# The landmark stage's first normalisations, turns and image 0's projections, moved into the last pair of the Fourier stage

## The chip, the cores and the metric

One Trainium2 chip, one core of it. The metric is the device time of one execution of the kernel in microseconds (us), as the median of several runs. The profile comes from one execution; its times count from the start of its span.

## The reference

```python
# x: (8, 16, 16, 192); a hybrid of four layers. Around the change:
x = x + _L1_conv_ref(_gn(x), ...)         # Fourier mixing of a group-normalised image
t = _to_tokens(x)                         # 8 images of 256 tokens, 192 channels
t = t + _L2_attn_ref(_ln_t(t), ...)       # landmark attention, per image

def _L1_conv_ref(x, w1, w2, b1, b2):
    xf = jnp.fft.rfft2(x, axes=(1, 2), norm='ortho')      # in 8 blocks of 24 channels
    o1 = softshrink(xf @ w1 + b1)                         # complex, block-wise
    o2 = softshrink(o1 @ w2 + b2)
    return irfft2(o2, s=(H, W), norm='ortho') + x

def _L2_attn_ref(x, Wqkv, bqkv, Wo, bo, Wconv):
    q, k, v = jnp.split(x @ Wqkv + bqkv, 3, axis=-1)      # 12 heads of 16
    q_l, k_l = pool(q), pool(k)                           # 16 landmarks: means over segments
    kernel_1 = softmax(q @ k_l.T * scale)
    kernel_2 = softmax(q_l @ k_l.T * scale)
    kernel_3 = softmax(q_l @ k.T * scale) @ v
    x_out = kernel_1 @ _iterative_pinv(kernel_2) @ kernel_3
    x_out = x_out + v_conv                                # depthwise, 33 taps along the tokens
    return x_out @ Wo + bo
```

`_ln_t` is a layer norm over the 192 channels without weights. Behind the landmark attention come a layer of routed experts, a full attention and another layer of experts.

## The kernel before

The kernel is a row of stages, each a block of instruction lists for the five engines: TensorE (PE), VectorE (DVE), ScalarE (ACT), GpSimd (POOL) and SyncE (SP, which issues most of the DMAs). At the end of a block all engines meet at a barrier, and nothing of the next block starts before it. Within a block each engine works through its list in order and waits on semaphores. The residual stream X, 8 images of 2 tiles of 128 tokens, stays in SBUF for the whole run.

**The Fourier stage**, `l1_afno`, takes the images in four pairs. In each, TensorE does `forward` (the transform), `first` and `second` (the two block-wise layers), `second_rest`, and `backward` (the inverse transform) of both images. ScalarE copies the spectrum (`spectrum`) and does the two halves of the first soft-shrink (`shrunk`). VectorE joins them (`hidden`), does the second soft-shrink (`result`, `result_rest`) and adds the residual (`residual`). Between these, the first three pairs carry the group-norm statistics of the pair to come: `gn.mean` and `gn.variance` on TensorE into the banks psM and psV, `gn.square` and `gn.root` on ScalarE, `gn.total` to `gn.norm` on VectorE. The last pair has none of this, and psM and psV lie unused in it. Behind each residual add stand the layer-norm statistics that the landmark attention needs, `stats.vector` (mean and variance, VectorE) and `stats.gpsimd` (the reciprocal root, GpSimd). GpSimd also makes the residual sum XS (L1689). SP loads the weights of the landmark stage (`early`) during this stage.

**The feature stage**, `l2_features`, runs over the images one by one as a software pipeline, c = -2 to 8 on TensorE and ScalarE. For each image: normalisation (`norm`, DVE L2098), turn (transposes, PE L1942) with a copy out (`turned_in`, ACT L2067), projections to queries, keys and values (PE L1953, L1960) with bias copies (`projected`, ACT L2046; `values`, DVE L2107), landmark means (`means`, DVE L2116 to L2121), logits (`logits`, PE L1970 and L1975), the convolution with rows of a Toeplitz matrix (`convolve`, PE L1990), softmaxes, and products. At c = -2 only image 0 is turned. At c = -1 image 0 is projected and image 1 is turned. At c = 0 image 1 is projected, and then come the logits of image 0. The order on TensorE is:

```python
for c in range(-2, B + 1):
    if has(c + 1): project(c + 1, queries)
    if has(c):     logits(c); convolve(c); turn_keys(c)
    if has(c + 2): turn(c + 2)
    if has(c):     landmarks(c)
```

The stage begins with SP's load of the Toeplitz rows `toep` (L1917), GpSimd's fills of the two value tiles VZ (L1924), and VectorE's `norm(0)`, `norm(1)` and the scaled head mask `hms` (L2153). Behind it come `l2_inverse` (the iterated inverse) and the route stage with the experts' weights. Each stage's semaphores are cleared by GpSimd at its end.

Of the kernel before, what the change touches and what calls it, by code (L numbers as in the profile page):

```python
# [17 lines left out]
T = HH * WW  # L18
P = 128
# [1622 lines left out]
def l1_afno(nc, G, w, consts, transfers, gn):  # L1642
# [5 lines left out]
    with Stage(nc, "l1") as st:  # L1648
# [8 lines left out]
        stats = LnStats(st, G, 1e-5)  # L1657
# [11 lines left out]
        def _(sp):  # L1669
# [8 lines left out]
            early.start(sp)  # L1678
            early.finish(sp)

        @block.gpsimd
        def _(pool):
            stats.init(pool)

# [13 lines left out]
            for u in range(2):  # L1698
                stats.gpsimd(nc, pool, B - 2 + u, u)

        @block.tensor
        def _(pe):
# [55 lines left out]
            for p in range(NP):  # L1758
                forward(2 * p)
                forward(2 * p + 1)  # L1760
                if p + 1 < NP:
                    gn.mean(pe, psM, p + 1)
                first(2 * p)
                first(2 * p + 1)
                if p + 1 < NP:
                    gn.variance(pe, psV, p + 1)
                second(2 * p)
                second(2 * p + 1)
                second_rest(p)
                backward(2 * p)  # L1770
                backward(2 * p + 1)

        @block.scalar
        def _(act):
# [18 lines left out]
            for p in range(NP):  # L1793
                spectrum(2 * p)
                spectrum(2 * p + 1)
                if p + 1 < NP:
                    gn.square(act, 2 * p + 2)
                    gn.square(act, 2 * p + 3)
                shrunk(2 * p, 0)
# [3 lines left out]
                if p + 1 < NP:  # L1803
                    gn.root(act, p + 1)

        @block.vector
        def _(dve):
# [31 lines left out]
            def residual(i):  # L1839
# [42 lines left out]
def l2_features(nc, G, w, consts, transfers):  # L1882
# [6 lines left out]
    with Stage(nc, "l2p") as st:  # L1889
        W, qkb, vb, hm = (G["marks"][n] for n in ("W", "qkb", "vb", "hm"))  # L1890
        hms = st.sb("hms", [CH, HB])
        toep = st.sb("toep", [P, NH, TW])
        two = lambda name, shape: [st.sb(f"{name}{u}", shape) for u in range(2)]
        xn, xT = two("xn", [P, TI, C]), two("xT", [CH, 2, T])
        QT, KT, VZ = two("QT", [CH, 2, T]), two("KT", [CH, 2, T]), two("VZ", [P, TI, NH, 2 * HD])
# [6 lines left out]
        normed, turned, xT_done, cleared, tp_in = st.sems("normed turned xT_done cleared tp_in")  # L1902
        q_mm, q_done, k_mm, k_done, v_mm, v_done, sum_done, lm_done = st.sems("q_mm q_done k_mm k_done v_mm v_done sum_done lm_done")
# [12 lines left out]
        def _(sp):  # L1916
            sp.dma_start(toep[:, :, :], rows(G["band"], 0, [TW, P], [P * TW, NH], [1, TW])).then_inc(tp_in, 16)  # L1917
# [13 lines left out]
        def _(pe):  # L1931
            reach = ((0, 0, P + KS // 2), (1, P - KS // 2, T))

            def turn(i):
                u = i % 2
                pe.wait_ge(normed, TI * (i + 1))
                if i >= 2:
                    pe.wait_ge(xT_done, i - 1)
                ps = both(psT[u][0:CH, :])
                for t in range(TI):  # L1940
                    for k in range(2):
                        mm = nc.tensor.transpose(ps[:, k, t * P:(t + 1) * P], xn[u][:, t, k * CH:(k + 1) * CH], ident[:, :])  # L1942
                mm.then_inc(turned, 1)

            def project(i, between):
                u = i % 2
                pe.wait_ge(xT_done, i + 1)
                for ps, m0, done, mm_done in ((psQ, 0, q_done, q_mm), (psK, 2, k_done, k_mm)):
                    if i:
                        pe.wait_ge(done, i)  # L1950
                    for a in range(2):
                        for k in range(2):
                            mm = nc.tensor.matmul(ps[0:CH, a * T:(a + 1) * T], W[:, k, (m0 + a) * CH:(m0 + a + 1) * CH], xT[u][:, k, :], start=(k == 0), stop=(k == 1))  # L1953
                    mm.then_inc(mm_done, 1)
                between()
                if i:
                    pe.wait_ge(v_done, i)
                for t in range(TI):
                    for k in range(2):
                        mm = nc.tensor.matmul(psV[:, t * C:(t + 1) * C], xT[u][:, k, t * P:(t + 1) * P], W[:, k, 2 * C:], start=(k == 0), stop=(k == 1))  # L1960
                mm.then_inc(v_mm, 1)
# [16 lines left out]
            def convolve(i):  # L1978
                u = i % 2
                if i == 0:  # L1980
                    pe.wait_ge(tp_in, 16)
# [40 lines left out]
            for c in range(-2, B + 1):  # L2022
# [9 lines left out]
                if has(c + 2):  # L2032
                    turn(c + 2)
# [4 lines left out]
        def _(act):  # L2038
            def projected(i):
                u = i % 2  # L2040
                if i >= 2:
                    act.wait_ge(l3_mm, i - 1)
                for ps, dst, b0, mm_done, done in ((psQ, QT, 0, q_mm, q_done), (psK, KT, 2, k_mm, k_done)):
                    act.wait_ge(mm_done, i + 1)
                    for a in range(2):
                        ev = nc.scalar.activation(dst[u][:, a, :], ps[0:CH, a * T:(a + 1) * T], ACT.Identity, bias=qkb[:, b0 + a:b0 + a + 1])  # L2046
                    ev.then_inc(done, 1)
# [14 lines left out]
            def turned_in(i):  # L2062
                u = i % 2
                act.wait_ge(turned, i + 1)
# [1305 lines left out]
```

## Time and profile before

| | us |
|---|---|
| median of 3 runs | 1144.66 |
| lowest and highest | 1143.66, 1145.24 |
| profiled execution | 1144.88 |
| its span | 1142.5 |
| TensorE busy | 1001.3 |
| VectorE busy | 579.1 |
| ScalarE busy | 420.7 |
| GpSimd busy | 286.9 |

The span reaches from the first to the last instruction of the profile; what lies around it is 2.4 us. A busy time is a sum over the engine's instructions. In rows of the profile, PEld is TensorE's load of weights, which overlaps its matmuls; PEclk is the clock granted to TensorE, 1.00 for 2.4 GHz and 0.50 for 1.2 GHz; an idle time in brackets names what ended it.

### The profile page before, as it was taken

How to read it: one execution, taken by the hardware profiler on the slowest of the kernel's cores; microseconds unless marked ns; L12 is line 12 of the kernel's file. 1: busy time of each engine (PE TensorE's matmuls, PEld its weight loads, DVE VectorE, ACT ScalarE, POOL GpSimd, SP SyncE). 2: the span in 40 equal slices, each digit the busy share in tenths (PEclk: the TensorE clock that was granted, in tenths of full speed). 3: DMA queues.
4: the chain of work that ended last, by engine and by line, in shares of the span. 5: the costliest groups of instructions: out<-in, count | busy, mean ns of one | idle time of the engine just before them, and what ended most of it. 6: DMA issues, size and time to landing. Idle time of an engine off the chain costs nothing. (4 is left out here: it accounts for less than half of the span.)

```text
span 1142.5 us, 20449 instructions
## 1 busy us (share of the span) xinstructions
PE 1001.3 (88%) x7506; PEld 760.0 (67%) x7507; DVE 579.1 (51%) x1394; ACT 420.7 (37%) x853; POOL 286.9 (25%) x399
## 2 busy tenths in 40 slices
PE   6796899999699999799799839999949799993996
PEld 5686687887457678688599715666637445573775
DVE  3754455554312375556475654444459487744221
ACT  3665055455332323344352101111107366641332
POOL 4464230111210021100000262555432311103242
PEclk9885899999799999899898859999979899995999
DMA  8543763330001220200003710111134443414670
GB/s 92 120 111 117 169 168 84 82 82 3 3 23 62 65 55 1 56 1 2 1 1 81 233 32 28 50 49 49 42 112 105 118 120 99 147 43 171 206 206 15
DMA packets 103318, 91.58 MB, mean 80 GB/s; under 512 B 25905, under 2 KB 95095, under 8 KB 102590
## 3 DMA queue, kind: packets, MB, share of 16 engines
q1 hardware_dynamic: 93161, 77.15, 25.2%
q0 software_dynamic: 5632, 11.07, 3.6%
q10 hardware_dynamic: 4437, 2.17, 0.7%
q8 instruction: 57, 0.93, 0.4%
q14 instruction: 31, 0.25, 0.1%
HBM read 64.44 MB, written 29.70 MB: 82 GB/s over the span
## 5 line engine op out<-in xcount | busy, mean ns | idle before, releaser
L1305 DVE TENSOR_REDUCE l0a_nmax<-l0a_psS 98x2 f32<-98x392 f32 x96 | 54.3, 567 | 54.9 <-PE l0a_psS L1120 50.8
L2778 ACT ACTIVATE l2e_H<-l2e_psH 128x512 f32<-128x512 f32 x40 | 21.7, 595 | 130.2 <-PE l2e_psH L2740 130.2
L895 ACT ACTIVATE l3a_PT<-l3a_psST 128x512 f32<-128x512 f32 x96 | 54.6, 595 | 31.5 <-PE l3a_psST L806 30.8
L1255 ACT ACTIVATE l0a_PT<-l0a_psST 98x392 f32<-98x392 f32 x96 | 47.2, 497 | 42.2 <-PE l0a_psST L1162 41.8
L2758 PEld LDWEIGHTS l2e_psY<-W2T,l2e_HT 128*128 128x128 f32 x320 | 51.5, 190 | 15.9 <-issue 15.8
L2701 POOL DMA_INDIRECT ys<-l2e_Y,result_of x40 | 42.0, 1050 | 72.3 <-DVE l2e_Y L2805 66.2
L2758 PE MATMUL l2e_psY<-W2T,l2e_HT 128*128 x320 | 57.3, 332 | 1.3 <-DVE l2e_Y L2805 0.8
L941 DVE TENSOR_REDUCE l3a_nmax<-l3a_psS 128x2 f32<-128x512 f32 x48 | 33.0, 687 | 24.6 <-PE l3a_psS L776 24.5
L2805 DVE COPY l2e_Y<-l2e_psY 128x384 f32<-128x384 f32 x20 | 11.2, 558 | 65.1 <-PE l2e_psY L2758 65.1
L2737 PE MATMUL l2e_psH<-W1T,l2e_XT 128*128 x80 | 41.3, 640 | 2.8 <-issue 2.0
L2696 POOL DMA_INDIRECT l2e_X<-xn,token_at x40 | 39.2, 980 | 17.1 <-issue 17.1
L806 PE MATMUL l3a_psST<-l3a_QS,l3a_KS 99*128 99x256 bf16 x192 | 36.4, 273 | 0.4 <-ACT l3a_PT L895 0.3
L941 DVE TENSOR_REDUCE l3a_nmax<-l3f_psL 128x2 f32<-128x512 f32 x48 | 32.8, 684 | 5.2 <-PE l3f_psL L776 5.2
L1257 ACT ACTIVATE l0a_PT<-l0a_psST 120x360 f32<-120x360 f32 x48 | 22.1, 470 | 31.8 <-PE l0a_psST L1170 29.3
L1554 PE MATMUL l0m_psY<-early,l0m_hT 128*128 128x192 f32 x192 | 32.2, 328 | 1.7 <-ACT l0m_hT L1584 1.7
L1308 DVE TENSOR_REDUCE l0a_nmax<-l0a_psS 120x1 f32<-120x312 f32 x48 | 22.9, 480 | 20.6 <-PE l0a_psS L1129 19.0
L1554 PEld LDWEIGHTS l0m_psY<-early,l0m_hT 128*128 128x128 f32 x192 | 31.1, 190 | 2.3 <-ACT l0m_hT L1584 2.3
L1087 POOL CAST l0a_mp<-l0a_nmax 128x20 bf16<-128x20 f32 x12 | 2.4, 199 | 120.0 <-DVE l0a_nmax L1308 120.0
L2974 PE MATMUL l3e_psY<-l3w_B,l3e_HT 128*128 128x192 f32 x192 | 32.5, 327 | 0.0
L1584 ACT ACTIVATE l0m_hT<-l0m_psH,early 128x512 f32<-128x512 f32 x24 | 15.2, 683 | 45.6 <-PE l0m_psH L1544 45.6
L1119 PE MATMUL l0a_psS<-l0a_KS,l0a_QS 96*98 96x196 bf16 x144 | 31.8, 258 | 0.0
L2974 PEld LDWEIGHTS l3e_psY<-l3w_B,l3e_HT 128*128 128x128 f32 x192 | 31.0, 190 | 0.3 <-issue 0.3
(575 smaller groups left out, 2719.6 us busy)
## 6 DMA issues: line engine op xcount, KB each, us to landing
l3w_A<-in_w SPq DMA_DIRECT2D x8, 771.0 KB, 4.9
l3w_B<-in_w SPq DMA_DIRECT2D x8, 672.0 KB, 5.5
l3a_QS<-qd SPq DMA_DIRECT2D x72, 64.0 KB, 2.2
l3a_KS<-kd SPq DMA_DIRECT2D x72, 64.0 KB, 2.3
rd<-l0q_r_p SPq DMA_DIRECT2D x24, 168.0 KB
l0a_QS<-qd SPq DMA_DIRECT2D x54, 64.0 KB
l0a_KS<-kd SPq DMA_DIRECT2D x54, 64.0 KB
W2T<-in_w2t SPq DMA_DIRECT2D x2, 1536.0 KB, 17.0
```

The costliest lines, as they stand in the source:

```text
L806: mm = nc.tensor.matmul(psST[item % 2][:, t * T:(t + 1) * T], KS[k % ring][:, s, key:key + P], QS[k % ring][:, s, u * T:(u + 1) * T], star ...
L895: nc.scalar.activation(PT[n % 3][:, s, :], psST[item % 2][:, :], ACT.Exp).then_inc(exp_done, 1)
L941: nc.vector.tensor_reduce(nmax[k % 2][:, TI * u:TI * (u + 1), s], psS[item % 2][:, :].rearrange("p (t k) -> p t k", t=TI), AX.X, ALU.max, ...
L1119: nc.tensor.matmul(o, q_[:, s, q], k_[:, s, keys], start=True, stop=False)
L1255: ex = nc.scalar.activation(PT[n % 3][0:WQ, s, :], psST[item % 2][0:WQ, 0:2 * W0], ACT.Exp)
L1305: mx = nc.vector.tensor_reduce(nmax[k % 2][0:WQ, 2 * j:2 * (j + 1), s], psS[item % 2][0:WQ, 0:2 * W0].rearrange("p (t k) -> p t k", t=2), ...
L1554: mm = nc.tensor.matmul(psY[a][:, t % 2 * C:(t % 2 + 1) * C], hT[p % 2][:, m, t * P:(t + 1) * P], Wd[:, m, :], start=(m == 0), stop=(m == ...
L2696: pool.indirect_dma_start(out=X[p % RING][:, t, :], out_offset=None, in_=G["xn"], in_offset=at(G["token_at"], 2 * p + t)).then_inc(x_in[p ...
L2701: pool.indirect_dma_start(out=G["ys"], out_offset=at(G["result_of"], 2 * p + t), in_=Y[p % RING][:, t, :], in_offset=None, bounds_check=2 ...
L2737: nc.tensor.matmul(psH[b][t][:, :], XT[b][:, t, :], W1T[:, 0, bass.ds(e * FI, FI)], start=True, stop=False)
L2758: mm = nc.tensor.matmul(psY[:, t * C:(t + 1) * C], HT[b][t][:, mb, :], W2T[:, bass.ds(e * NM + mb, 1), :].rearrange("p a c -> p (a c)"), s ...
L2974: mm = nc.tensor.matmul(psY[t][:, 0:C], HT[b][:, m, t * P:(t + 1) * P], W2[e][:, m, :], start=(m == 0), stop=(m == MF - 1))
```

## The change

A new class, `LandmarkFront`, owns the tiles and semaphores of the landmark attention's first steps and outlives both stages. With it:

- VectorE normalises images 0 and 1 and scales the mask in the last pair of the Fourier stage, behind the residual add of image 5.
- TensorE turns both images behind `forward`, projects image 0's queries behind `first`, and its values and keys behind `second_rest`. The banks are psM, psV and psB[1][1].
- ScalarE copies the turns out and makes the bias copies of queries and keys; VectorE adds the values' bias ahead of the residual of image 6.
- GpSimd fills the value tiles at the Fourier stage's start, and SP loads the Toeplitz rows behind the early weights.
- The layer-norm statistics of image 7 move to the feature stage: on VectorE behind `means(0)` and `norm(2)`, on GpSimd first. `norm(7)` waits for them.
- The feature stage begins at c = 0 with the projections of image 1.
- `W1T` and `W2T` are allocated ahead of these stages, and the tile D of `l2_inverse` takes the place of the Toeplitz rows. Neither alters an instruction's work.

```diff
 def l1_afno(...):                      # the Fourier stage
-        stats = LnStats(st, G, 1e-5)
+        stats = lf.stats
 SP:
             early.start(sp)
+            lf.load_taps(sp)
             early.finish(sp)
+            sp.wait_ge(lf.tp_in, 16)
 GpSimd:
             stats.init(pool)
+            lf.clear_values()
...
-            for u in range(2):
-                stats.gpsimd(nc, pool, B - 2 + u, u)
+            stats.gpsimd(nc, pool, B - 2, 0)
 TensorE, in the loop over pairs p:
                 forward(2 * p + 1)
                 if p + 1 < NP:
                     gn.mean(pe, psM, p + 1)
+                else:
+                    lf.turn(pe, 0, psM)
+                    lf.turn(pe, 1, psV)
                 first(2 * p)
                 first(2 * p + 1)
                 if p + 1 < NP:
                     gn.variance(pe, psV, p + 1)
+                else:
+                    early.finish(pe)
+                    pe.wait_ge(lf.xT_done, 1)
+                    lf.project_queries(psM, 0)
                 second(2 * p)
                 second(2 * p + 1)
                 second_rest(p)
+                if p + 1 == NP:
+                    lf.project_values(psB[1][1], 0)
+                    pe.wait_ge(lf.xT_done, 2)
+                    lf.project_keys(psV, 0)
                 backward(2 * p)
                 backward(2 * p + 1)
 ScalarE:
                     gn.square(act, 2 * p + 3)
+                else:
+                    lf.turned_in(act, 0, psM)
                 shrunk(2 * p, 0)
...
+            lf.turned_in(act, 1, psV)
+            lf.queries(act, 0, psM)
+            lf.keys(act, 0, psV)
 VectorE:
-                stats.vector(nc, dve, i, i % 2, (x_done, i + 1))
+                if i < B - 1:
+                    stats.vector(nc, dve, i, i % 2, (x_done, i + 1))
...
                 if p:
                     residual(2 * p - 1)
+                if p + 1 == NP:
+                    dve.wait_ge(stats.kept, 4)
+                    lf.norm(dve, 0)
+                    lf.norm(dve, 1)
+                    early.finish(dve)
+                    lf.scaled_mask()
...
+                else:
+                    dve.wait_ge(lf.cleared, 2)
+                    lf.values(dve, 0, psB[1][1])
                 residual(2 * p)

 def l2_features(...):                  # the feature stage
 SP:
-            sp.dma_start(toep[:, :, :], rows(G["band"], ...)).then_inc(tp_in, 16)
 GpSimd:
-            for u in range(2):
-                nc.gpsimd.memset(VZ[u][:], 0.0).then_inc(cleared, 1)
+            lf.stats.gpsimd(nc, pool, B - 1, (B - 1) % 2)
 TensorE and ScalarE:
-            for c in range(-2, B + 1):
+            for c in range(B + 1):
 VectorE:
-            norm(0)
-            norm(1)
-            nc.vector.tensor_scalar(hms[:, :], hm[:, :], ...).then_inc(cleared, 1)
-            dve.wait_ge(cleared, 3)
-            for c in range(-1, B + 1):
+            dve.wait_ge(lf.cleared, 3)
+            means(0)
+            lf.norm(dve, 2)
+            lf.stats.vector(nc, dve, B - 1, (B - 1) % 2)
+            for c in range(B + 1):
...
                 if has(c + 3):
-                    norm(c + 3)
+                    if c + 3 == B - 1:
+                        dve.wait_ge(lf.stats.kept, B + 2)
+                    lf.norm(dve, c + 3)
```

The methods of `LandmarkFront` hold the code of the feature stage's functions of the same names, for instance:

```python
def norm(self, dve, i):
    if i >= 2:
        dve.wait_ge(self.turned, i - 1)
    for t in range(TI):
        k = TI * i + t
        self.nc.vector.tensor_scalar(self.xn[i % 2][:, t, :], G["X"][:, k, :], G["MEAN"][:, k:k + 1], G["RSTD"][:, k:k + 1], ALU.subtract, ALU.mult).then_inc(self.normed, 1)

def turn(self, pe, i, bank):
    pe.wait_ge(self.normed, TI * (i + 1))
    ...
    for t in range(TI):
        for k in range(2):
            mm = self.nc.tensor.transpose(ps[:, k, t * P:(t + 1) * P], self.xn[u][:, t, k * CH:(k + 1) * CH], self.G["ident"][:, :])
    mm.then_inc(self.turned, 1)
```

## Rows read from the trace of the kernel before

**Rows 1.** The page, first part: busy us, share of the span, instructions of each engine.

```profile
PE 1001.3 (88%) x7506; PEld 760.0 (67%) x7507; DVE 579.1 (51%) x1394; ACT 420.7 (37%) x853; POOL 286.9 (25%) x399
```

**Rows 2.** Busy time by stretches: start:end, length, busy us (instructions) of each engine, clock, DMA.

```profile
387.00:403.00 16.00, 15.08 (x102) 12.93 (x101) 7.54 (x17) 5.96 (x15) 2.03 (x3) 1.00 0.15 50
...
435.00:451.00 16.00, 16.00 (x98) 12.51 (x97) 8.81 (x25) 4.40 (x11) 3.78 (x6) 1.00 0.01 3
...
464.00:480.00 16.00, 14.34 (x65) 11.14 (x66) 5.37 (x20) 5.79 (x11) 0.92 (x2) 0.81 0.38 99
...
480.00:500.00 20.00, 19.68 (x197) 16.05 (x196) 12.81 (x36) 9.03 (x23) 1.83 (x2) 1.00 0.00 1
```

**Rows 3.** Timeline of the boundary: start us, duration us, engine, line, instruction, idle before it.

```profile
460.13 0.56 DVE L1842 TENSOR_TENSOR X<-l_psY,l_XS 128x384 f32<-128x384 f32 x1 [1.24 <-PE l_psY L1755]
...
462.01 0.71 POOL L163 TENSOR_TENSOR RSTD<-l_stat_ve,l_stat_exponent 128x2 f32<-128x2 f32 x1
...
463.07 2.24 DVE L2098 TENSOR_SCALAR l2p_xn<-X,MV,RSTD 128x192 f32<-128x192 f32 x4 [1.45 <-PEq L77]
...
463.36 1.56 POOL L1924 MEMSET l2p_VZ<- 128x768 f32 x2 [0.63 <-POOLq L77]
...
464.30 1.09 PE L1942 MATMUL l2p_psT<-ident,l2p_xn 128*96 128x128 f32 x4 [4.21 <-DVE l2p_xn L2098]
...
466.07 2.96 PEld L1953 LDWEIGHTS l2p_psQ<-l2p_xT,early 96*96 96x96 f32 x8 [1.11 <-ACT l2p_xT L2067]
```

**Rows 4.** Busy time by single microseconds around the boundary.

```profile
463.00:464.00 1.00, 0.00 (x0) 0.00 (x0) 0.93 (x2) 0.00 (x0) 0.65 (x1) 0.58 0.00 0
...
469.00:470.00 1.00, 1.00 (x3) 0.59 (x3) 0.00 (x0) 0.16 (x1) 0.00 (x0) 0.51 0.82 199
...
470.00:471.00 1.00, 1.00 (x6) 0.78 (x5) 0.00 (x0) 0.67 (x2) 0.00 (x0) 1.00 0.01 3
```

**Rows 5.** Timeline of the feature stage's start, images 0 and 1.

```profile
472.66 0.51 PEld L1942 LDWEIGHTS l2p_psT<-ident,l2p_xn 128*96 128x96 f32 x4
...
473.76 0.67 DVE L2116 TENSOR_REDUCE l2p_sums<-l2p_QT 96x32 f32<-96x512 f32 x1
...
474.10 1.54 PEld L1953 LDWEIGHTS l2p_psQ<-l2p_xT,early 96*96 96x96 f32 x8 [0.94 <-ACT l2p_xT L2067]
...
475.42 0.35 DVE L2121 TENSOR_TENSOR l2p_klbd<-l2p_sums,l2p_hms 96x192 f32<-96x192 f32 x1
...
476.11 0.83 ACT L2046 ACTIVATE l2p_QT<-l2p_psQ,early 96x256 f32<-96x256 f32 x2 [2.06 <-PE l2p_psQ L1953]
...
478.77 1.02 PEld L1970 LDWEIGHTS l2p_ps<-l2p_klbd,l2p_QT 96*128 96x128 f32 x8
...
479.13 0.75 DVE L2107 TENSOR_TENSOR l2p_VZ<-l2p_psV,early 128x96 f32<-128x96 f32 x4 [2.79 <-PE l2p_psV L1960]
```

**Rows 6.** Timeline of the feature stage: a normalisation beside GpSimd.

```profile
484.41 1.17 DVE L2098 TENSOR_SCALAR l2p_xn<-X,MV,RSTD 128x192 f32<-128x192 f32 x2
```

**Rows 7.** Timeline of the Fourier stage's last pair.

```profile
446.51 0.41 PEld L1722 LDWEIGHTS l_psB<-l1g_FX,l1g_W 97*96 97x96 f32 x2
...
448.85 0.46 DVE L1818 TENSOR_TENSOR l1g_C<-l_UP,l_DN 96x288 f32<-96x288 f32 x1 [4.45 <-ACT l_DN L1789]
```

**Rows 8.** DMA issues: out<-in, queue, count, size, median us to landing.

```profile
l2p_toep<-band SPq DMA_DIRECT2D x1, 960.0 KB, 5.7
```

**Rows 9.** Timeline of the boundary into the Fourier stage.

```profile
389.01 0.56 DVE L1624 TENSOR_TENSOR X<-l0m_psY,X 128x384 f32<-128x384 f32 x1 [3.34 <-PE l0m_psY L1554]
...
389.89 1.91 PE L1711 MATMUL l_psB<-early,l1g_XN 128*96 128x288 f32 x7 [0.92 <-PEq L77]
```

**Rows 10.** Busy time by stretches at the route stage's end and the experts' start.

```profile
660.00:680.00 20.00, 4.30 (x40) 2.93 (x41) 12.31 (x23) 1.28 (x1) 12.76 (x13) 0.50 0.09 23
...
680.00:700.00 20.00, 17.96 (x69) 8.68 (x67) 6.09 (x13) 3.26 (x6) 4.30 (x5) 0.87 0.10 29
```

More of the change, by code:

```diff
@@ L1639, in afno_tiles, with l1_afno @@
     return [(t["ones"], consts["gnones"]), (t["DF"], consts["dft"]), (t["IV"], consts["idft"]), (t["IVB"], consts["idftb"])]
-def l1_afno(nc, G, w, consts, transfers, gn):
+def l1_afno(nc, G, w, consts, transfers, gn, lf):
     with Stage(nc, "l1") as st:
@@ L1889, in l2_features @@
+def l2_features(nc, G, w, consts, transfers, lf):
     with Stage(nc, "l2p") as st:
-        W, qkb, vb, hm = (G["marks"][n] for n in ("W", "qkb", "vb", "hm"))
-        hms = st.sb("hms", [CH, HB])
-        toep = st.sb("toep", [P, NH, TW])
+        hm = G["marks"]["hm"]
+        hms, toep, QT, KT, VZ = lf.hms, lf.toep, lf.QT, lf.KT, lf.VZ
         two = lambda name, shape: [st.sb(f"{name}{u}", shape) for u in range(2)]
-        xn, xT = two("xn", [P, TI, C]), two("xT", [CH, 2, T])
-        QT, KT, VZ = two("QT", [CH, 2, T]), two("KT", [CH, 2, T]), two("VZ", [P, TI, NH, 2 * HD])
@@ L1932, in _ @@
             reach = ((0, 0, P + KS // 2), (1, P - KS // 2, T))
[L1934 to L1943, printed above, removed]
-            def project(i, between):
[L1946 to L1954, printed above, removed]
-                between()
[L1956 to L1961, printed above, removed]
+            def project(i, between):
+                pe.wait_ge(lf.xT_done, i + 1)
+                pe.wait_ge(q_done, i)
+                lf.project_queries(psQ, i)
+                pe.wait_ge(k_done, i)
+                lf.project_keys(psK, i)
+                between()
+                pe.wait_ge(v_done, i)
+                lf.project_values(psV, i)
             def logits(i):
@@ L2032, in _ @@
                 if has(c + 2):
-                    turn(c + 2)
+                    lf.turn(pe, c + 2, psT[c % 2])
                 if has(c):
@@ L2039, in projected @@
             def projected(i):
-                u = i % 2
                 if i >= 2:
                     act.wait_ge(l3_mm, i - 1)
[L2043 to L2047, printed above, removed]
+                lf.queries(act, i, psQ)
+                lf.keys(act, i, psK)
             def exps(i):
@@ L2076, in queries_back @@
                 nc.scalar.activation(K1T[:, :, i * T:(i + 1) * T], both(ps1[0:CH, :]), ACT.Copy).then_inc(k1_done, 1)
-            for c in range(-2, B + 1):
+            for c in range(B + 1):
                 if has(c + 1):
@@ L2177, in l2_inverse @@
         WIDE = CH + LM
-        U, U2, D = (st.sb(n, [CH, NG, WIDE]) for n in ("U", "U2", "D"))
+        U, U2, D = *(st.sb(n, [CH, NG, WIDE]) for n in ("U", "U2")), spare
         S = st.sb("S", [CH, NG, LM])
@@ L3331, in build @@
         net.window_attention()
-        with Stage(nc, "l1g") as across:
-            gn = FourierFront(across, net.G)
-            net.window_mlp(gn)
-            net.fourier(gn)
-        net.landmark_attention()
+        net.routing()
+        with Stage(nc, "l2g") as beyond:
+            lf = LandmarkFront(beyond, net.G)
+            with Stage(nc, "l1g") as across:
+                gn = FourierFront(across, net.G)
+                net.window_mlp(gn)
+                net.fourier(gn, lf)
+            net.landmark_attention(lf)
         with Stage(nc, "l2y") as between:
```

119 lines of the change are left out of this document (83 added, 36 removed).

## The prediction

> **What bounds the kernel now.** I began with the page. TensorE is busy for 88% of the span, more than any other engine [rows 1], so time comes off where TensorE stands still or runs slowly. Then I took the busy time by stretches around the change [rows 2]. In 435 to 451 us, inside the Fourier stage, TensorE is busy for all 16.00 us. In 464 to 480, the start of the feature stage, it is busy for only 14.34 of 16, and the granted clock is 0.81. In 480 to 500 it is dense again, 19.68 of 20 at clock 1.00. The boundary is the weak place, and both stages beside it are paced by TensorE.
>
> The timeline of the boundary shows why [rows 3]. The last residual add of the Fourier stage starts at 460.13. Behind it come the statistics of image 7, which end on GpSimd at 462.01 + 0.71 = 462.72. Only then does the feature stage start (463.07), with four normalisations; TensorE's first turn comes at 464.30, after 4.21 us with nothing to do, and image 0's query projection at 466.07. By single microseconds the clock is 0.58 in 463 to 464 and 0.51 in 469 to 470, and 1.00 from 470 [rows 4]: it fell during TensorE's idle time and came back some 4 us after dense work resumed. The low level (1.2 GHz) thus lies on image 0's projections. From 474.10 everything is dense [rows 5].
>
> The marker for the sum is the first weight load of image 0's logits (L1970), at 478.77. From there on both kernels do the same work in the same order. From residual add to marker is 478.77 - 460.13 = 18.64 us, with these parts:
> - residual add 0.56
> - image 7's statistics, up to 462.72: 2.03
> - the barrier, to 463.07: 0.35
> - first normalisation, until TensorE turns at 464.30: 1.23
> - turn of image 0, its copy out, hand-over, to 466.07: 1.77
> - query, key and value projections of image 0, to 472.66: 6.59
> - turn of image 1 and its copy out, to 474.10: 1.44
> - projections of image 1, to 478.77: 4.67
>
> **The change part by part.**
>
> Image 7's statistics: 2.03 us leave the path. They move behind the means of image 0 and the normalisation of image 2 on VectorE, in the feature stage. VectorE is done with the means by 475.42 + 0.35 = 475.77, which is 2.0 us after their start at 473.76 [rows 5]. Started at the barrier, means 2.0, normalisation at most 1.17 [rows 6] and statistics at most 2.03 make 5.2 us. The next thing that VectorE has to do is image 1's values, which waits for a projection at 4.67. So at most 0.5 us is late, on a step that precedes nothing urgent: TensorE works on the logits for more than that before it needs the values. I take 0. Image 7 is normalised four images later.
>
> The first four normalisations: they go to the head of the last pair's VectorE work, behind the residual add of image 5. There VectorE sits idle for 4.45 us before 448.85 [rows 7]. Four of them took 2.24 us at the boundary, beside GpSimd's fills [rows 3]; the mask scaling is a few tenths more. They start at about 444.4 and end by 446.7. TensorE reaches the turns at 446.51 [rows 7] and the second turn half a microsecond later, so both images are ready in time. Without that cover they would cost up to 2.3.
>
> In the place considered, GpSimd makes its two residual sums at the same time. The row of a pair beside GpSimd is 1.17 us; the 2.24 for four agrees with it [rows 3, 6]. The Trainium skill, GPSIMD Engine Reference, section 1 (Specifications), says that GpSimd shares its SBUF interfaces with VectorE and contends with its two-port modes and with instructions of two SBUF inputs; that rule speaks against putting them here. By it and by the row alike the normalisations need 2.3 instead of some 1.3 us, still under 4.45, and the sum is unchanged.
>
> TensorE's added work: TensorE has no gap in the last pair that could absorb it [rows 2], so each load and matmul moved there lengthens the Fourier stage. Two turns cost 0.5 each (four loads, 0.51 [rows 5]); image 0's three projections cost what image 1's do at full clock, 4.67. Together 5.7 us. From below: a hand-over gap that the new work fills may give back 0.3, so 5.4. From above: five new waits on TensorE (two on the normalisations, one on the early transfers, two on ScalarE's copies) are not in the trace. The nearest row is the 1.44 from turn to projection, of which 0.5 is the turn [rows 5]: 0.9 for a copy that nothing covers. If one is uncovered the sum is 6.6. The copy of image 0 is covered by the eight first-layer groups, the copy of image 1 by the second layer, so I take 5.7.
>
> ScalarE gets two copies, each of at most the 0.9 above, and two pairs of bias copies of 0.83 [rows 5]. Between its spectrum copies and its last shrink it is paced by TensorE, and the four bias copies lie behind all its Fourier work and beside the inverse transform. VectorE's value adds (0.75 [rows 5]) are put in front of the residual of image 6, which waits for the inverse transform of image 6; that starts only after the key projection. Both at 0. If they were uncovered they would cost under 1 us.
>
> GpSimd's two fills of the value tiles (1.56 [rows 3]) now precede its first residual sum. That sum is needed only when the pair's inverse transform is done, a whole pass of TensorE later, so 0. The Toeplitz rows (960 KB, 5.7 us to land [rows 8]) are issued behind the early loads on SP's queue, early in the Fourier stage, with nothing behind them there. At the boundary SP's queue loses one issue before the two loads of the later attention. Nobody waits for either: 0.
>
> The barrier: after the change it is VectorE that comes last, not GpSimd. The nearest row of that form is the boundary into the Fourier stage: VectorE ends at 389.01 + 0.56 = 389.57 and TensorE starts at 389.89, so 0.32 [rows 9]. Other clearings of semaphores move to a later boundary, at most 0.2.
>
> The clock: in the changed kernel TensorE idles over the boundary from its last matmul to the next start: before, that matmul ended at 464.30 - 4.21 = 460.09, 0.04 ahead of the residual add, so 0.04 + 0.56 + 0.32 = 0.92 us instead of 4.21. At the boundary into the Fourier stage it idles 0.92 us too [rows 9], and the clock of the 16 us around it is 1.00 [rows 2]. I take full clock. The Trainium skill, TensorE: Matmul & The Clock Gate, Part 1, says that the throttled state is the default and activity releases it; the trace agrees in direction [rows 4].
>
> **The sum.** After: 5.7 (added) + 0.56 + 0.32 + 4.67 (image 1's projections) = 11.25 us, against 18.64. The gain is 7.4 us. The profiled execution took 1144.88 us (span 1142.5 and 2.4 around it), so 1137.5. It lies 0.2 above the median of the runs, so the predicted time is 1137.3 us, faster by 0.65%.
>
> **The rivals.**
> - *The clock falls all the same.* For it: the idle time doesn't vanish. Against it: the 0.92 us of [rows 9] and the clock of 1.00 in [rows 2] inside the Fourier stage. Price: image 0's projections took 6.59 in the spell against 4.67, so 1.9, and up to 4.7 if the whole of image 1's ran at the low level. Time 1139.2 to 1142.0. Chance 8%.
> - *An uncovered hand-over in the Fourier stage*: TensorE waits for the second normalisation or for a copy, 0.9 to 2.3 us. Time 1138.2 to 1139.6, centre 1139. Chance 13%.
> - *More comes off*: the marker itself moves by more since later stretches profit from the earlier or warmer start. One spell less on the route stage's edge would give 2 to 3 us, 1135 or below. Chance 8%.
> - *Slower: the clock's spells behind the stage meet other work.* In 660 to 680 the clock is 0.50 with TensorE busy for 4.30 us, and in 680 to 700 it is 0.87 with TensorE busy for 17.96 [rows 10]. If such a spell stayed where it is while the work came 7.4 us earlier, 7.4 us of work at half rate would lose 3.7. Two such edges cancel the gain (1144.7), three make it 1148.4. Against it: the spell at the boundary began and ended with TensorE's own idle and dense time [rows 4], so spells should move along, and the three runs lie within 1.6 us. Chance of no gain or a loss 5% (slower by over 0.2%: 3%).
> - *Nothing moves at all* would need something other than TensorE to pace the last pair, which [rows 2] excludes; it is inside the 5%.
>
> The remaining 66% is my forecast itself, 1136 to 1138.5. The range reaches from 1135.2, so that a part of the third rival is in, to 1140.3, which takes in the second and half of the first: about 8 in 10. A change within 0.2% (2.3 us) is about what this measurement cannot tell from none. Faster 0.93, same 0.04, slower 0.03.
>
> **What would show it.** In the changed profile: the Fourier stage's last residual add at about 465.8; no statistics between it and the barrier; TensorE idle for 0.9 to 1.3 us at the boundary, clock 1.00 throughout; the query projection of image 1 as the first work of the feature stage at about 466.7; the logits' first load at about 471.4. No wait of TensorE in the last pair above 0.3 us. I am wrong if the added work there takes over 6.7 us, if the clock shows a spell below 1 around 467 to 472, or if the shift at the marker (7.4) isn't found again at the end of the run.

## The result, and the profile after

In the first measurement the changed kernel took 1133.38 us (median; 1131.43 to 1135.65, 4 runs) against 1144.78 (1143.66 to 1145.24, 4 runs): a ratio of 0.9903, interval 0.9881 to 0.9925. Forecast were 1137.3 us, 1135.2 to 1140.3. So the change is faster, and by 11.4 us instead of 7.4.

Two repetitions with unaltered copies gave 0.9942 (0.9925 to 0.9958) and 0.9911 (0.9889 to 0.9933). Over all measurements of this study the mean of the kernel before is 1143.5 (122 runs, 1136.8 to 1148.4) and that of the changed kernel 1134.2 (14 runs, 1129.8 to 1136.1), 9.4 us apart. A single execution strays by several us, which the three runs shown ahead of the prediction had hidden. One execution of a kernel below, 1157.2 us in before_pad33, fell in a slower state of the chip (mean granted clock 0.907) and is left out of means and comparisons.

The page after:

```profile
span 1129.5 us, 20453 instructions
...
PE 992.3 (88%) x7506; PEld 754.4 (67%) x7507; DVE 578.6 (51%) x1394; ACT 420.3 (37%) x853; POOL 286.5 (25%) x399
```

The last pair of the Fourier stage after, on the timeline (start us, duration, engine, line, instruction, idle before it):

```profile
443.67 0.56 DVE L1860 TENSOR_TENSOR X<-l_psY,l_XS 128x384 f32<-128x384 f32 x1
...
445.08 1.61 DVE L1940 TENSOR_SCALAR l2g_xn<-X,MV,RSTD 128x192 f32<-128x192 f32 x4
...
447.28 0.59 PEld L1950 LDWEIGHTS l_psM<-ident,l2g_xn 128*96 128x96 f32 x4
...
447.85 0.45 PEld L1950 LDWEIGHTS l_psV<-ident,l2g_xn 128*96 128x96 f32 x4
...
450.49 0.46 DVE L1836 TENSOR_TENSOR l1g_C<-l_UP,l_DN 96x288 f32<-96x288 f32 x1 [3.72 <-ACT l_DN L1802]
...
452.19 1.58 PEld L1963 LDWEIGHTS l_psM<-l2g_xT,early 96*96 96x96 f32 x8
```

These answer to [rows 7]. The normalisations take 1.61 us in VectorE's idle time, and the two turns start at 447.28 and 447.85. VectorE still has 3.72 us of idle time ahead of its next join (450.49), and TensorE doesn't wait; image 0's queries follow the first layer at 452.19.

The end of the pair, and the boundary, which answer to [rows 3, 5]:

```profile
457.88 1.27 PEld L1976 LDWEIGHTS l_psB<-early,l2g_xT 96*128 96x128 f32 x8
...
460.79 0.73 PEld L1754 LDWEIGHTS l_psY<-l_C,early 128*128 128x128 f32 x4
...
466.48 0.56 DVE L1860 TENSOR_TENSOR X<-l_psY,l_XS 128x384 f32<-128x384 f32 x1 [1.24 <-PE l_psY L1757]
...
467.48 1.54 PEld L1963 LDWEIGHTS l2p_psQ<-l2g_xT,early 96*96 96x96 f32 x8 [1.33 <-issue]
467.51 1.94 PE L1963 MATMUL l2p_psQ<-l2g_xT,early 96*96 96x256 f32 x8 [1.06 <-PEq L77]
...
469.07 1.67 PEld L1963 LDWEIGHTS l2p_psK<-l2g_xT,early 96*96 96x96 f32 x8
...
470.80 1.38 PEld L1976 LDWEIGHTS l2p_psV<-early,l2g_xT 96*128 96x128 f32 x8
...
472.15 1.02 PEld L2067 LDWEIGHTS l2p_ps<-l2p_klbd,l2g_QT 96*128 96x128 f32 x8
```

The last residual add starts at 466.48, 22.81 us behind image 5's (443.67). Before it was 17.23, from this row to 460.13 [rows 3]:

```profile
442.90 0.56 DVE L1842 TENSOR_TENSOR X<-l_psY,l_XS 128x384 f32<-128x384 f32 x1
```

So 5.58 us were added, where the sum had 5.7. TensorE is idle for 1.06 us, and image 1's projections start at 467.48. The marker, the first load of image 0's logits, stands at 472.15, 5.67 us behind the residual add, where the sum had 0.56 + 0.32 + 4.67 = 5.55 and the kernel before 18.64.

By stretches of 16 us, which answer to [rows 2]:

```profile
451.00:467.00 16.00, 15.44 (x93) 12.41 (x91) 6.80 (x19) 4.35 (x11) 0.93 (x2) 1.00 0.00 0
467.00:483.00 16.00, 15.33 (x128) 12.72 (x129) 10.16 (x32) 7.67 (x18) 1.84 (x3) 1.00 0.15 38
```

The clock is 1.00 over the boundary. From image 5's residual add to the marker the changed kernel takes 472.15 - 443.67 = 28.48 us, the kernel before 478.77 - 442.90 = 35.87. That is 7.39 less, the forecast. But the spans differ by 1142.5 - 1129.5 = 13.0 us. Of those, -0.8 came ahead of the marker's stretch (the changed kernel reached image 5's residual add later), 7.4 in it and 6.4 behind it. By the prediction's own last sign of being wrong, the shift at the marker isn't found again at the end of the run. The question is what happens behind the marker.

### The profile page after: what moved, and what is told of

It reads as the page before. It is cut to its first block and busy times, and to the rows that moved or that the text cites. A ratio compares the mean times of both kernels' runs of the same rounds, so it can differ in the third digit from the quotient of the medians.

```text
span 1129.5 us, 20453 instructions
## 1 busy us (share of the span) xinstructions
PE 992.3 (88%) x7506; PEld 754.4 (67%) x7507; DVE 578.6 (51%) x1394; ACT 420.3 (37%) x853; POOL 286.5 (25%) x399
## 5 line engine op out<-in xcount | busy, mean ns | idle before, releaser
L1584 ACT ACTIVATE l0m_hT<-l0m_psH,early 128x512 f32<-128x512 f32 x24 | 15.2, 683 | 45.6 <-PE l0m_psH L1544 45.6
```

## The experiments

Each profile was cut at three points: image 5's residual add, the marker, and the first instruction of the inverse stage (l2i_mx), which is the end of the feature stage:

```profile
566.02 0.42 DVE L2250 TENSOR_REDUCE l2i_mx<-K2L 96x16 f32<-96x256 f32 x1 [0.66 <-PEq L77]
...
556.11 0.42 DVE L2323 TENSOR_REDUCE l2i_mx<-K2L 96x16 f32<-96x256 f32 x1 [0.66 <-PEq L77]
```

The first is of the kernel before, the second of the changed one. A spell is a stretch of time in which the granted clock of TensorE is 0.50. The padded kernels have n transposes of the identity ahead of image 0's logits, on TensorE, at full clock.

| kernel | add of image 5 to marker | marker to stage end | stage end to end | mean of times (runs) |
|---|---|---|---|---|
| before, 1st profile | 35.87 | 87.25 | 576.5 | |
| before_again | 35.94 | 87.23 | 576.2 | 1143.2 (10) |
| before_third | 35.92 | 87.25 | 575.8 | 1144.1 (12) |
| changed, 1st profile | 28.48 | 83.96 | 573.4 | 1133.5 (4) |
| after_again | 28.48 | 83.96 | 576.3 | 1135.6 (4) |
| after_third | 28.51 | 83.96 | 577.7 | 1133.7 (6) |
| after_pad33 | 32.16 | 83.91 | 576.7 | 1137.9 (10) |
| after_pad38 | 32.68 | 85.54 | 574.6 | 1142.0 (12) |
| after_pad42 | 33.12 | 83.91 | 580.6 | 1143.8 (12) |
| after_pad66 | 35.74 | 83.91 | 577.7 | 1141.9 (10) |
| before_pad27 | 38.89 | 83.92 | 573.1 | 1145.9 (12) |
| before_pad33 | 39.50 | 87.19 | 582.7 | 1145.9 (11) |
| stats_back | 32.23 | 83.97 | 576.7 | 1137.8 (9) |
| proj_back | 28.37 | 85.59 | 577.6 | 1133.5 (6) |
| before_stats_later | 34.61 | 83.96 | 573.8 | 1136.9 (6) |
| before_warm | 33.50 | 83.96 | 578.3 | 1142.8 (12) |

The first three columns are from one execution each, and the last is over all its runs. The profile of before_pad33 is that of its execution of 1157.2 us, so of its last part (582.7) nothing is concluded. A profile shows which spells one execution met, not which the others met. Those of the kernel before are of executions of 1144.88, 1146.20 and 1145.93 us, all above the kernel's mean of 1143.5.

### The two kernels again, and the changed one put back

No edit in after_again, before_again, after_third and before_third. The padded ones have, in l2_features on TensorE:

```diff
+                if c == 0:
+                    for _ in range(66):          # 33 in the other
+                        nc.tensor.transpose(ps1[:, 0:P], ident[:, :], ident[:, :])
                 if has(c):
                     logits(c)
```

> The changed kernel once more, unaltered. Theory A (the change is worth 7.4 us at the marker, and the 4 us beyond it come from where TensorE's spells at the low clock fall behind the marker, which differs between executions and with any shift): the marker again 7.4 us closer to image 5's residual add than before (28.5 us behind it against 35.9), the time between 1131 and 1137, and the spells behind the marker begin at other points of the work than in the first profile, so that the stretch from marker to end differs by over 0.5 us. Theory B (the change itself speeds the later stages): the same marker, and the stretch from marker to end within 0.3 us of the first profile's.

> The kernel before once more, unaltered. Theory A: the marker lies where it lay, and low-clock spells begin at other points of the work than in the first profile; the time may leave 1143.7 to 1145.2 by up to 2 us to either side. Theory B: times again within 1143.7 to 1145.2 and the same spells on the same work.

> The changed kernel with 66 transposes of the identity (into a bank that is still free) ahead of image 0's logits, which keep TensorE dense and put everything behind the marker back by some 7.3 us, to where it lay in the kernel before. Theory A: the gain behind the marker is no property of the change: time about 1133.4 + 7.3 = 1140.7 on average but free to lie anywhere between 1139 and 1146, near 1144.8 if the spells depend on when the work arrives since the start. Theory B: 1140.7 within 0.7, since the stages behind keep their gain.

> The same with 33 transposes, 3.6 us. Theory A: time not in line between the changed kernel and the one with 66: it may be off 1137.0 by 1 to 3 us, since each spell behind the marker gains or loses busy time of its own. Theory B: 1137.0 within 0.7.

The 28.48 us to the marker came again to the hundredth. The changed kernel took 1135.52 us (ratio 0.9942), before_again 1143.01 (1.0001). Marker to end was 660.2 us instead of 657.4, over 0.5 us apart as theory A wanted. For the kernel before it was 663.4 instead of 663.7, with the same spell on the last image: there theory A's shifted spells didn't come. And the table has something that neither theory had: marker to stage end is 83.96 in both profiles of the changed kernel and 87.2 in both of the kernel before, 3.3 us more, for the same instructions.

With 33 transposes the time was 1137.57 (0.996, 0.9945 to 0.9975), with 66 it was 1142.07 (0.999, 0.997 to 1.001). By means that is 3.7 and 7.8 us over the changed kernel's 1134.2, for 3.7 and 7.3 us of work. Theory B wanted 1137.0 and 1140.7 within 0.7; the medians are 0.6 and 1.4 off, so these two don't part the theories. They fit that the 7.4 us are worth about 7.4 in the time.

The profile of after_pad66 says more. It has the marker 35.74 us behind image 5's add, within 0.2 of where the kernel before has it, and still marker to stage end is 83.91. So the place of the marker behind image 5's add doesn't by itself bring the spell.

### Where the 3.3 us lie

> The kernel before, unaltered, a third profile. Theory A with arrival alike in each execution: the spell on the last image of the feature stage is there again, and marker to end takes 663 to 664 us. If spells fall at random over executions, it is there in about one of three.

> The changed kernel, unaltered, a third profile and more times. Local gain at the marker 7.4 us as twice before; no spell inside the feature stage; marker to end 657 to 661 us. The ratio of the times, with more runs, says how much of the whole the 7.4 us are: 0.9935 if they are all of it, 0.990 with 4 us beyond them.

In before_third the 87.25 came a third time; in after_third the 83.96 and a time of 1134.61 (0.9911). Marker to end was 661.6 us in after_third, 0.6 above the 657 to 661 expected. Here is the end of the feature stage in before_third, by windows of 5 us (TensorE's busy time first, the clock third from the end):

```profile
555.00:560.00 5.00, 3.97 (x18) 2.76 (x17) 1.75 (x5) 0.91 (x2) 0.35 (x1) 0.72 0.01 3
560.00:565.00 5.00, 4.64 (x53) 3.25 (x52) 1.61 (x4) 2.00 (x7) 0.84 (x1) 0.60 0.00 0
```

and TensorE's weight loads in it:

```profile
556.79 1.44 PEld L1970 LDWEIGHTS l2p_ps<-l2p_klbd,l2p_QT 96*128 96x128 f32 x8 [1.00 <-issue]
...
560.10 3.56 PEld L1990 LDWEIGHTS l2p_psC<-l2p_toep,l2p_VZ 128*32 128x32 f32 x48 [0.70 <-issue]
```

The same work in the changed kernel, by windows and by loads:

```profile
545.00:550.00 5.00, 3.46 (x28) 2.95 (x28) 2.09 (x8) 1.05 (x3) 0.84 (x1) 1.00 0.01 3
550.00:555.00 5.00, 4.40 (x70) 3.64 (x68) 2.42 (x7) 2.51 (x7) 0.84 (x1) 1.00 0.00 0
```

```profile
548.34 0.97 PEld L2067 LDWEIGHTS l2p_ps<-l2p_klbd,l2g_QT 96*128 96x128 f32 x8 [1.00 <-issue]
...
550.27 1.87 PEld L2087 LDWEIGHTS l2p_psC<-l2g_toep,l2g_VZ 128*32 128x32 f32 x48 [0.36 <-issue]
```

The loads of the last image's logits (L1970 before, L2067 after) take 1.44 against 0.97 us, those of the convolution (L1990, L2087) 3.56 against 1.87. The idle time ahead of the logits' first load is 1.00 us in both. In before_third the clock is 0.72 and 0.60 in the two windows, in the changed kernel 1.00. So the same idle time was followed by a low-clock spell in three of three executions of the kernel before and in none of three of the changed one.

### The kernel before, put back

The edit is that of the padded kernels, with 27 and 33 transposes, in the kernel before.

> The kernel before with 27 transposes of the identity ahead of image 0's logits: 3.0 us of work more, at the full clock. In both profiles of the kernel before a spell at the low clock lies on the last image's logits and convolution (6.8 us of busy TensorE); in none of the seven altered kernels does one begin just there. Theory A (which spells the work behind the marker meets depends on when it arrives, and arrives in much the same place in each execution of one kernel): put back by 3.0 us the work misses that spell, as it does in the changed kernel, so the feature stage ends within 0.8 us of where it ended, for 3 us more of work, and the time is within 1.5 us of before. Theory B (the change itself removed that spell): the spell stays, stage end and time 3.0 us later.

> The same with 33 transposes, 3.6 us. Theory A: no fixed expectation for the spell on the last image; either it is there, and the stage ends 3.6 us later, or not, and it ends 0.4 us later. Theory B: 3.6 us later. Time 1143.5 + 3.6 = 1147.1 in B.

With 27 the marker came 2.97 us later (38.89 against 35.92) and the spell was gone: marker to stage end 83.92. So the stage ended 0.4 us earlier than without the 3 us of extra work (38.89 + 83.92 against 35.92 + 87.25). Its rows (marker, stage end):

```profile
482.12 0.97 PEld L1970 LDWEIGHTS l2p_ps<-l2p_klbd,l2p_QT 96*128 96x128 f32 x8
...
566.04 0.42 DVE L2253 TENSOR_REDUCE l2i_mx<-K2L 96x16 f32<-96x256 f32 x1 [0.66 <-PEq L77]
```

Nothing of the change is in that kernel, so the spell can go without the change, and theory B falls for the 3.3 us of the profiles. The times are less clear. The median was 1146.03 against 1144.69, ratio 1.0019 (1.0001 to 1.0038): inside theory A's 1.5 us, but the interval, 0.1 to 4.3 us, holds B's 3.0 and not the 0.4 less that the profile suggests. The profiled execution, 1141.44 us, was the fastest of its twelve, whose mean is 1145.9; whether the others missed the spell isn't known. With 33 the spell was there (87.19), and the ratio 1.0014 (0.9992 to 1.0036), -0.9 to 4.1 us: that fits both theories.

### The changed kernel, put back to the spell

> The changed kernel with 38 transposes of the identity ahead of image 0's logits, 4.2 us more; with 33 of them marker to stage end took 83.9 us, without the spell. Theory A (arrival time alone): somewhere between 34 and 45 transposes the work arrives as the kernel before does and meets the spell on the last image, so marker to stage end jumps to 87.2, and the time rises by 4.2 + 3.3 = 7.5 over the changed kernel, to that of the kernel before. Theory B (the changed kernel is free of that spell by itself): 83.9, time 4.2 above the changed kernel.

> The same with 42 transposes, 4.6 us more. Theory A: marker to stage end 87.2 here or with 38, in at least one of the two; time up to 7.9 above the changed kernel. Theory B: 83.9, 4.6 above.

With 38 a spell came, but a shorter one, on the last convolution and not on the logits ahead of it: marker to stage end 85.54, not 87.2.

```profile
550.00:555.00 5.00, 4.19 (x34) 2.92 (x37) 2.79 (x7) 1.57 (x4) 0.00 (x0) 0.79 0.00 0
555.00:560.00 5.00, 4.28 (x56) 3.31 (x50) 0.94 (x5) 1.60 (x7) 0.84 (x1) 0.87 0.00 0
```

With 42 there was none in the profiled execution. The 87.2 us were met in neither, so that expectation of theory A missed. The times speak for it all the same: by means 1142.0 and 1143.8, that is 7.8 and 9.6 us over the changed kernel, for 4.2 and 4.6 us of work. Theory B had 4.2 and 4.6. From 33 transposes (1137.9) to 38 the mean rises by 4.1 us for 0.5 us of work. The two were measured apart; each against the kernel before in its own measurement they are 5.2 and 0.9 us faster, a rise of 4.2. The profiles don't explain it: that of after_pad38 is of the second fastest of its twelve executions (1137.26). With 38 and 42 the kernel is as slow as the kernel before (0.9997, 0.9981 to 1.0014, and 1.0007, 0.9987 to 1.0027).

### The parts of the change

stats_back: image 7's statistics back in the Fourier stage.

```diff
-                if i < B - 1:
-                    stats.vector(nc, dve, i, i % 2, (x_done, i + 1))
+                stats.vector(nc, dve, i, i % 2, (x_done, i + 1))
...
-            stats.gpsimd(nc, pool, B - 2, 0)
+            for u in range(2):
+                stats.gpsimd(nc, pool, B - 2 + u, u)
... in l2_features
-            lf.stats.gpsimd(nc, pool, B - 1, (B - 1) % 2)
...
-            lf.stats.vector(nc, dve, B - 1, (B - 1) % 2)
```

> The changed kernel with image 7's statistics back at the end of the Fourier stage, the rest of the change kept. My sum says that they are worth 2.0 us there: last residual add to marker 5.67 + 2.0 = 7.7 us, TensorE idle for 2.9 us over the boundary instead of 1.0. Rival (the clock): with that idle time TensorE may drop to its low level, which costs image 1's projections another 1.9 to 2.4 us, 9.6 to 10.1 in all. Rival (nothing): other work hides the statistics, 5.7.

Last residual add to marker was 9.42 us: between the sum's 7.7 and the rival's 9.6. The timeline and the windows of this kernel show the rival, nearly whole:

```profile
465.85 0.56 DVE L1861 TENSOR_TENSOR X<-l_psY,l_XS 128x384 f32<-128x384 f32 x1 [1.24 <-PE l_psY L1758]
...
468.94 2.44 PE L1963 MATMUL l2p_psQ<-l2g_xT,early 96*96 96x256 f32 x8 [3.13 <-PEq L77]
...
470.75 3.11 PEld L1963 LDWEIGHTS l2p_psK<-l2g_xT,early 96*96 96x96 f32 x8
...
473.92 1.38 PEld L1976 LDWEIGHTS l2p_psV<-early,l2g_xT 96*128 96x128 f32 x8
```

```profile
470.00:472.00 2.00, 2.00 (x7) 1.32 (x6) 1.46 (x6) 0.57 (x2) 0.00 (x0) 0.56 0.91 252
472.00:474.00 2.00, 2.00 (x7) 1.38 (x6) 0.00 (x0) 0.26 (x1) 0.00 (x0) 0.59 0.13 28
```

TensorE was idle for 3.13 us. Image 1's keys took 3.17 us from first load to the values' (470.75 to 473.92), against 1.73 in the changed kernel (469.07 to 470.80), at a clock of 0.56 and 0.59. Of the 3.75 us that the statistics cost here (9.42 - 5.67), 2.07 are TensorE's longer idle time (3.13 against 1.06) and 1.7 its work at the low clock. The time was 1137.41 (0.9948, 0.9933 to 0.9963), by means 3.6 over the changed kernel.

proj_back: image 0's projections and their bias work back at the head of the feature stage. The diff shows TensorE's part; ScalarE's bias copies and VectorE's value adds move with it.

```diff
                 else:
-                    early.finish(pe)
-                    pe.wait_ge(lf.xT_done, 1)
-                    lf.project_queries(psM, 0)
+                    pass
...
-                if p + 1 == NP:
-                    lf.project_values(psB[1][1], 0)
-                    pe.wait_ge(lf.xT_done, 2)
-                    lf.project_keys(psV, 0)
... in l2_features, TensorE
+            pe.wait_ge(lf.xT_done, 1)
+            lf.project_queries(psQ, 0)
+            lf.project_keys(psK, 0)
+            lf.project_values(psV, 0)
             for c in range(B + 1):
```

> The changed kernel with image 0's projections back at the head of the feature stage; normalisations, turns, fills, Toeplitz rows and later statistics stay changed. My sum says that moving projections at full clock from one dense place to another is worth nothing: marker within 0.5 us of the changed kernel's 28.5 behind image 5's residual add, since the 4.67 us that leave the Fourier stage return in the feature stage. Rival (the projections are the gain): 4.7 us later, 33.2. A third way: the copy and bias work of ScalarE, or the values' adds ahead of the means on VectorE, hold up the logits, 1 us later.

The marker came at 28.37, where the changed kernel has 28.48 (a short spell on later work shows as 85.59 in the next column), and the time was 1134.86 (0.9905, 0.9879 to 0.9931; mean 1133.5). Moving 4.67 us of projections is worth nothing; the sum's reading stands, and both rivals fall.

before_stats_later: the kernel before, with the statistics of image 7 alone moved.

```diff
-                stats.vector(nc, dve, i, i % 2, (x_done, i + 1))
+                if i < B - 1:
+                    stats.vector(nc, dve, i, i % 2, (x_done, i + 1))
... GpSimd
-            for u in range(2):
-                stats.gpsimd(nc, pool, B - 2 + u, u)
+            stats.gpsimd(nc, pool, B - 2, 0)
... in l2_features, GpSimd, behind its fills
+            stats.gpsimd(nc, pool, B - 1, (B - 1) % 2)
... in l2_features, VectorE
                 if has(c + 3):
+                    if c + 3 == B - 1:
+                        dve.wait_ge(stats.kept, B + 2)
                     norm(c + 3)
+                if c == -1:
+                    stats.vector(nc, dve, B - 1, (B - 1) % 2)
```

> The kernel before with one part of the change alone: image 7's statistics behind the normalisation of image 2 in the feature stage. My sum: 2.0 us off the stretch from the last residual add to the marker (18.64), so 16.6, and TensorE idle for 2.2 us instead of 4.2. If the low-clock spell goes with the idle time, another 2.4 less, 14.2. Rival: VectorE's later statistics hold up the values of image 0, and part of the 2.0 comes back.

Last residual add to marker was 17.39, 1.25 us less and not 2.0:

```profile
460.08 0.56 DVE L1840 TENSOR_TENSOR X<-l_psY,l_XS 128x384 f32<-128x384 f32 x1 [1.24 <-PE l_psY L1753]
...
460.96 2.24 DVE L2098 TENSOR_SCALAR l2p_xn<-X,MV,RSTD 128x192 f32<-128x192 f32 x4 [0.32 <-PEq L77]
...
462.19 0.64 PE L1942 MATMUL l2p_psT<-ident,l2p_xn 128*96 128x128 f32 x4 [2.14 <-DVE l2p_xn L2098]
...
466.61 3.27 PEld L1953 LDWEIGHTS l2p_psK<-l2p_xT,early 96*96 96x96 f32 x8
...
470.00 1.38 PEld L1960 LDWEIGHTS l2p_psV<-early,l2p_xT 96*128 96x128 f32 x8
```

The stage began 2.1 us earlier, but the spell stayed, with TensorE idle for 2.14 us. The earlier work then lay deeper in it: image 0's keys took 3.39 us from first load to the values' (466.61 to 470.00). So part of the gain went back to the clock, not to VectorE's later statistics, which stood behind the values of image 0. The whole kernel took 1136.99 (0.994, 0.9921 to 0.9959), by means 6.6 us less than before. At the marker 1.3 of them are seen, in the feature stage 3.3, since the spell on the last image is gone here too (83.96), and behind it 2.0 to 2.7 (573.8 against 575.8 to 576.5).

before_warm: the kernel before, TensorE kept at work over the boundary.

```diff
                 backward(2 * p + 1)
+            for _ in range(22):
+                nc.tensor.transpose(psM[:, 0:P], G["ident"][:, :], G["ident"][:, :])
... in l2_features
+            for _ in range(10):
+                nc.tensor.transpose(ps1[:, 0:P], ident[:, :], ident[:, :])
             for c in range(-2, B + 1):
```

> The kernel before with TensorE kept at work over the boundary: 22 transposes of the identity behind its last inverse transform and 10 ahead of its first turn, both in time in which it had nothing to do. My price of the low-clock spell on image 0's turn and projections is 1.9 + 0.5 = 2.4 us: residual add to marker 18.64 - 2.4 = 16.2 with clock 1.00 throughout. Rival (the spell comes anyway, or the projections are slow for another reason, such as the Toeplitz load beside them): 18.6.

```profile
464.00:468.00 4.00, 3.32 (x22) 2.51 (x21) 2.14 (x5) 0.59 (x1) 1.56 (x2) 1.00 0.80 215
468.00:472.00 4.00, 3.81 (x22) 3.07 (x20) 0.53 (x4) 1.82 (x5) 0.00 (x0) 1.00 0.80 180
```

The clock stayed at 1.00, and last residual add to marker took 16.28 us, 2.4 less than 18.7, with the Toeplitz load beside the projections all the same. That is the price of the spell, as worked out. In the time little of it is seen: 1142.02 (0.999, 0.9974 to 1.0005). Its profile gives 3.3 us in the feature stage too, and then the longest way but two from stage end to end, 578.3.

### The last part, from stage end to end

The same traces show what makes this part long or short. I added up TensorE's busy time, matmuls and weight loads, inside the spells behind the feature stage. It is 53.3, 49.4 and 50.3 us in the three profiles of the kernel before, 46.9, 52.3 and 52.6 in those of the changed one, and 46.9 to 55.9 over the fifteen profiles without before_pad33's. Work at half the clock takes about twice its time (the convolution's loads above, 3.56 against 1.87 us), so half of this sum is an estimate of what the spells cost. With that half taken off, stage end to end is 548.7 to 552.6 us in these fifteen, where it was 573.1 to 580.6. So the part differs mainly by how much work lies in spells, and hardly by anything in the kernels.

In its first profile the changed kernel gains 3.1 us here, and 2.3 of these lie in one stretch: from the first load of the route stage's logits (l2r_psL) to the first of the experts' (l2e_psH) it takes 45.6 us (622.5 to 668.1), the kernel before 47.9 (631.6 to 679.4), and the changed kernel's later profiles 47.7 and 47.9.

## Why the prediction was wrong

The shift at the marker was right. Wrong was the step from there to the end, which put the rest of the run at no difference. Point by point, by its steps:

- **Image 7's statistics, 2.03 us: right in the sum, incomplete as a price.** Alone in the kernel before they bring 1.25 us at the marker, since the spell stays; put back into the changed kernel they cost 3.75, since they bring a spell.
- **The normalisations, hidden: right.** 1.61 us beside GpSimd, under the 2.3 allowed, and no wait of TensorE.
- **TensorE's added work, 5.7 us: right.** 5.58.
- **The barrier 0.32 and TensorE's idle time 0.92: near.** Image 1's projections start 1.0 us behind the last residual add's start, not 0.88; TensorE is idle for 1.06. This 0.12 too much and the 0.12 too little in the added work cancel, so that the marker comes right to the hundredth is in part luck.
- **The clock over the boundary: right.** 1.00 in the changed kernel; before_warm measures the spell at 2.4 us, as the sum has it (1.9 + 0.5).
- **Projections moved at no gain, values and bias copies at 0: right.** proj_back.
- **The marker, 7.4 us nearer: right.** 7.39, and within 0.1 in each later pair of profiles.
- **"From there on both kernels do the same work in the same order", and "spells should move along": the step that failed.** The work is the same, but not its clock. Between the marker and the end of the feature stage the kernel before meets a spell that costs 3.3 us, in three profiled executions of three; the changed kernel meets none in three, and the kernel before met none in the one profiled once it was put back by 3.0 us. The rival "slower" had that mechanism, spells that meet other work, with the other sign and at 5%. The rival "more comes off" had the sign, and 2 to 3 us at the route stage's edge, at 8%; there 2.3 us came off in the first profile and none in the later two. I had argued from one spell, whose fall and rise lay beside an idle and a dense stretch of TensorE, to all; the end of this stage shows the same idle time with a fall and without.
- **The range.** It was built around three runs within 1.6 us. The kernel before strays over 11.6 us in 122 runs, so an error of 1 to 2 us in a median of four runs is to be had without any cause in the kernel. With 7.4 at the marker and 3.3 in the stage, 10.7 would be expected of the whole; the medians of the first measurement say 11.4, the means of all runs 9.4. Either way the changed kernel lies below the range. If some executions of the kernel before miss the spell, the 3.3 us count for less than that in its mean; one profile per measurement can't tell.

Behind the feature stage no mean difference between the two kernels is to be seen. That part took 573.4 to 577.7 us in the three profiles of the changed kernel and 575.8 to 576.5 in those of the one before. The first profile of the changed kernel owes 3.1 of its 13.0 us to it, and the two later ones owe it +0.2 and -1.2 against the first profile of before.

Open is what decides whether the last image's work in the feature stage meets the spell. It isn't the change (before_pad27), nor the idle time ahead of the logits alone (1.00 us in both), nor how far behind image 5's add the marker comes (after_pad66). Open too is why 38 and 42 transposes cost 4 to 5 us more than their work. One execution of after_pad42 (1143.02 us, near its mean) shows a long last part, 580.6, with 55.9 us of TensorE's work in spells; the profile of after_pad38 is of one 4.7 us below its mean.

## What to carry to other kernels

A step that is moved is worth the waits and the low-clock work that it takes with it, not its own busy time: here hand-overs, statistics and one spell made 7.4 us, and 4.67 us of moved projections nothing. Cut both traces at the same instruction behind the change before judging a sum; what differs behind that point needs a cause of its own. Where TensorE's clock falls several times in a run, a shift of later work can change which work the spells meet: here that was 3.3 us in one stage, and some us to either side belong in the range.

## What the runs showed of the hardware

Half a microsecond of added work cost 4.1 us in the mean (after_pad33 to after_pad38, 10 and 12 runs), and 3.0 us of added work cost 1.3 by medians (before_pad27, interval 0.1 to 4.3). Idle times of TensorE of 1.06 us (changed), 2.14 (before_stats_later), 3.13 (stats_back) and 4.21 (before) at this boundary went with no spell, one, one and one. The fall need not lie in the idle time: in before it did (463 to 464, clock 0.58), in stats_back the clock was still 1.00 from 469 to 470, when TensorE had resumed at 468.94, and 0.62 from 470 to 471. At the end of the feature stage one gap of 1.00 us and its neighbours were followed by a spell in all three profiles of the kernel before and in none of the changed kernel, for the same instructions.
